# Expert layers: another router arithmetic, a first tile picked and last tiles joined on TensorE

## What is computed

```
# first mixture (L0): a router with a hidden layer, experts 512 -> 2048 -> 512
logits = silu(x @ rw1 + rb1) @ rw2 + rb2
k_prob = softmax(top_k(logits, 2))
out = sum_e we[e] * (silu(x @ w1[e] + b1[e]) @ w2[e] + b2[e])
# second mixture (L1): router_logits = x @ router_w + router_b, experts 512 -> 512 -> 512
ff_out = (silu(x @ we_gate[e]) * (x @ we_up[e])) @ we_down[e]
```

## Time and profile before

| | us |
|---|---|
| median of 3 runs | 2418.44 |
| lowest, highest | 2414.98, 2419.09 |
| the profiled execution's own time | 2414.82 |
| its span, first to last instruction | 2412.8 |
| TensorE busy | 2134.6 |
| TensorE's mean granted clock | 0.948 |

### The profile page before, as it was taken

The page is one execution under the profiler, slowest core; times in us unless marked ns, Lnnn a source line. Parts: engine busy times, 40 slices in busy tenths (PEclk is TensorE's granted clock), DMA queues, the critical chain, the costliest instruction groups (busy, mean ns, idle before and its releaser), DMA issues. The chain is left out here.

```text
span 2412.8 us, 37208 instructions
## 1 busy us (share of the span) xinstructions
PE 2134.6 (88%) x14521; PEld 1599.3 (66%) x14521; DVE 1382.4 (57%) x2318; ACT 1331.3 (55%) x2560; POOL 296.6 (12%) x268
## 2 busy tenths in 40 slices
PE   6999999999968957799999949999999999765895
PEld 4778787777735533278888736887787877532674
DVE  4455455454536651189999944544555545454686
ACT  2566566565624422088888824666665665401684
POOL 3111112121010000100000022121121121101001
PEclk9999999999988988799999969999999999978898
DMA  4010101010020013499999640010101010013896
GB/s 148 18 36 19 36 19 36 19 36 19 2 107 0 1 43 147 151 360 355 365 354 362 254 157 22 33 36 19 36 19 36 19 36 1 1 70 114 311 351 225
DMA packets 52220, 263.85 MB, mean 109 GB/s; under 512 B 9288, under 2 KB 9672, under 8 KB 25040
## 3 DMA queue, kind: packets, MB, share of 16 engines
q1 hardware_dynamic: 45168, 245.23, 27.4%
q0 software_dynamic: 2560, 8.39, 1.1%
q10 hardware_dynamic: 4320, 7.87, 0.9%
HBM read 244.42 MB, written 17.04 MB: 108 GB/s over the span
## 5 line engine op out<-in xcount | busy, mean ns | idle before, releaser
L508 DVE COPY c_pt<-bank 128x512 f32<-128x512 f32 x256 | 177.0, 692 | 548.9 <-PE bank L342 548.8
L658 ACT ACTIVATE c_pr<-wide,c_nmax 128x512 f32<-128x512 f32 x512 | 348.9, 696 | 164.7 <-DVE c_nmax L500 83.9
L231 POOL TENSOR_TENSOR c_clo<-c_raw,c_chi 128x512 fp32r<-128x512 f32 x128 | 167.3, 1311 | 991.9 <-ACT c_chi L635 991.9
L342 PE MATMUL bank<-ident,c_pr 128*128 128x128 f32 x2048 | 268.6, 273 | 13.9 <-DVE c_pt L508 11.8
L342 PEld LDWEIGHTS bank<-ident,c_pr 128*128 128x128 f32 x2048 | 238.0, 140 | 49.9 <-DVE c_pt L508 14.0
L92 PE MATMUL bank<-c_wv_hi,c_chi 128*128 128x512 f32 x512 | 218.4, 426 | 20.1 <-POOL c_clo L231 18.8
L643 ACT ACTIVATE c_khi<-bank,c_cols 128x512 fp32r<-128x512 f32 x128 | 87.9, 687 | 252.1 <-PE bank L94 252.1
L1535 DVE TENSOR_TENSOR moe_wlo<-moe_raw,moe_whi 128x2048 fp32r<-128x2048 f32 x97 | 219.4, 2286 | 12.7 <-ACT moe_whi L1426 12.5
L92 PE MATMUL bank<-c_chi,c_wk_hi 128*128 128x512 f32 x512 | 213.6, 417 | 8.7 <-ACT c_v L649 8.6
L1426 ACT CAST moe_whi<-moe_raw 128x2048 fp32r<-128x2048 f32 x97 | 185.3, 1931 | 37.0 <-DMA moe_raw<-in_L_ffn_w 14.2
L93 PE MATMUL bank<-c_wv_lo,c_chi 128*128 128x512 f32 x512 | 203.2, 397 | 0.0
(11 more groups left out here) (320 smaller groups left out, 3877.4 us busy)
## 6 DMA issues: line engine op xcount, KB each, us to landing
moe_hr<-in_L_ffn_w SPq DMA_DIRECT2D x68, 1024.0 KB, 7.2
moe_raw<-in_L_ffn_w SPq DMA_DIRECT2D x52, 1024.0 KB, 7.2
c_raw<-in_ctx SPq DMA_DIRECT2D x32, 1024.0 KB, 4.9
moe_raw<-in_L_ffn_we_gate SPq DMA_DIRECT2D x15, 1024.0 KB, 7.2
moe_raw<-in_L_ffn_we_up SPq DMA_DIRECT2D x15, 1024.0 KB, 7.5
moe_raw<-in_L_ffn_we_down SPq DMA_DIRECT2D x15, 1024.0 KB, 7.0
slot_outputs<-moe_ob ACTq DMA_DIRECT2D x30, 256.0 KB, 7.4
ret_w<-in_L_attn_w_attn SPq DMA_DIRECT2D x4, 1024.0 KB, 9.1
```

The source lines that it names most:

```text
L231: nc.gpsimd.tensor_tensor(clo[:, g % 2, c, :], raw[:, c, :], f32(chi[:, g % 2, c, :]), ALU.subtract) \
L342: last = pe.transpose(TB[n % 2][:, h * P:(h + 1) * P], pr[:, u % 2, h, n * P:(n + 1) * P], k["ident"][:])
L508: nc.vector.tensor_copy(pt[:, n, :], TB[0][:]).then_inc(pt_dve, 1)
L658: nc.scalar.activation(pr[:, u % 2, h, :], S[h][:], ACT.Exp, bias=nmax[:, b % 2, i, at:at + 1], scale=-1.0 if masked else 1.0, accum_out=d ...
```

## The change

- The zero rows of `slot_rows` are written in the retention stage, behind its own loads.
- First layer's router: `rw1` comes in four 1 MB parts among the first expert blocks; it and the turned rows are split into rounded part and remainder, and each full-precision matmul becomes three one-pass products (`hidden`).
- Logits: `rw2` is laid into columns padded from 8 to 32, and four hidden pieces are multiplied in four column groups of TensorE (`to_logits`), in the first layer four times, three of these between the hidden products. Four matmuls with a 0/1 matrix `fold` then add the groups and turn the result; the bias is added behind that.
- First tile: 0/1 matrices `here` (128 tokens by 128 slots) are made on VectorE and 16 full-precision matmuls put the first tile's turned rows straight into `XB` (`place_first`). The other 14 tiles still go through DRAM.
- Last tiles (`LATE`: one in the first layer, two in the second): their outputs stay in `ob`. GpSimd makes a matrix with each pair's probability at its slot, TensorE turns it in the loop (`turn_late`), and behind the loop full-precision matmuls with it add these tiles to the tokens (`join_late`), in the first layer with the b2 product. The gather takes only the earlier tiles (`EARLY`) and doesn't wait for the last; a pair of a late tile gathers row 0 with probability 0.
- VectorE's and TensorE's steps for b2 move from ahead of the first layer's loop into it.

```diff
                 sp.dma_start(wp[:], t["L0_attn_w_proj"]).then_inc(S["wp_in"], 16)
+                sp.wait_ge(S["zero"], 1)
+                sp.dma_start(slots.rearrange("(i p) d -> p i d", p=P), zero[:].to_broadcast([P, slots.shape[0] // P, D])) \
+                    .then_inc(S["zeroed"], 16)
+                sp.wait_ge(S["zeroed"], 16)
...
+    LATE = 1 if first else 2
+    EARLY = NT - LATE
...
+        RWN = 48 if first else 32
+        CHUNK = ((1, 3), (3, 7), (7, NT))
...
+                    rw1_of = t["L0_ffn_rw1"].rearrange("p c (g h) -> p g c h", g=GR)
+                    sp.dma_start(rw1[:, 0], rw1_of[:, 0]).then_inc(r1_in[0], 16)
...
-                    sp.dma_start(rw1, t["L0_ffn_rw1"]).then_inc(s_["rw_in"], 16)
+                    sp.dma_start(rw1[:, 1], rw1_of[:, 1]).then_inc(r1_in[1], 16)
...
+                    load(0)
+                    sp.dma_start(rw1[:, 2], rw1_of[:, 2]).then_inc(r1_in[2], 16)
+                    load(1)
+                    sp.dma_start(rw1[:, 3], rw1_of[:, 3]).then_inc(r1_in[3], 16)
                     sp.dma_start(b1[:], t["L0_ffn_b1"]).then_inc(s_["b_in"], 16)
                     sp.dma_start(b2[:], t["L0_ffn_b2"]).then_inc(s_["b_in"], 16)
+                    load(2)
+                    sp.wait_ge(s_["logits_made"], 1)
...
-                if first:
-                    sp.wait_ge(s_["filled"], 1)
-                    sp.dma_start(xg.rearrange("(i p) d -> p i d", p=P), hr[:, 0:1, :].to_broadcast([P, NT, D])) \
-                        .then_inc(s_["zeroed"], 16)
...
-                    sp.dma_start(rows_in[:, a:b, :], xg[a * P:b * P, :].rearrange("(i p) d -> p i d", p=P)).then_inc(xg_in[i], 16)
+                    sp.dma_start(rows_in[:, a - 1:b - 1, :], xg[a * P:b * P, :].rearrange("(i p) d -> p i d", p=P)).then_inc(xg_in[i], 16)
...
+                pool.wait_ge(s_["filled"], 1)
+                pool.wait_ge(s_["rw_in"], RWN)
+                nc.gpsimd.tensor_copy(rw2_wide[:, :, 0:NE], rw2[:]).then_inc(s_["wide"], 1)
...
+                pool.wait_ge(s_["scattered"], 16 * 2 * NB)
+                pool.wait_ge(x_turned, 1)
+                pool.wait_ge(s_["probs"], 1)
+                for l in range(LATE):
+                    for b in range(NB):
+                        for i, to in enumerate((late_of, late_2nd)):
+                            nc.gpsimd.tensor_scalar(to[:, l, b * P:(b + 1) * P], in_late[:, l, :], slot_f[:, b, i:i + 1],
+                                                    prob[:, b, i:i + 1], ALU.is_equal, ALU.mult).then_inc(s_["late_parts"], 1)
+                pool.wait_ge(s_["late_parts"], 2 * NB * LATE)
+                nc.gpsimd.tensor_tensor(late_of, late_of, late_2nd, ALU.add).then_inc(s_["late_made"], 1)
+                pool.wait_ge(od_done[0], 16 * ((EARLY + 1) // 2))
+                pool.wait_ge(od_done[1], 16 * (EARLY // 2))
...
-                    nc.gpsimd.indirect_dma_start(out=back[:, i, :], out_offset=None, in_=od,
-                                                 in_offset=bass.IndirectOffsetOnAxis(ap=slot_i[:, i:i + 1], axis=0)) \
+                    nc.gpsimd.indirect_dma_start(out=back[:, i, :], out_offset=None, in_=od[0:EARLY * P, :],
+                                                 in_offset=bass.IndirectOffsetOnAxis(ap=back_i[:, i:i + 1], axis=0)) \
...
+                def hidden(j):
+                    g, q = j // C, j % C
+                    if q == 0:
+                        pe.wait_ge(rlo_done, g + 1)
+                    after(pe, s_["h_read"], j - 1)
+                    for c in range(C):
+                        at = c * D + q * P
+                        last = three_products(pe, ps[4 + j % 2][:], whi[1][:, g % 2, at:at + P], wlo[1][:, g % 2, at:at + P],
+                                              xT_hi(c), xT_lo(c), c == 0, c == C - 1)
+                    last.then_inc(s_["h_made"], 1)
+
+                def to_logits(rows, g, n):
+                    if first:
+                        pe.wait_ge(s_["h_read"], C * (g + 1))
+                    for q in range(C):
+                        last = pe.matmul(ps[6][q * HD:(q + 1) * HD, :], rw2_wide[:, C * g + q, :], rows[:, C * g + q, :],
+                                         start=(g == 0), stop=(g == n - 1))
+                    return last
+
...
+                        hidden(j)
+                        if j == 2 * C - 1:
+                            pe.wait_ge(s_["wide"], 1)
+                        if j % C == C - 1 and j > C:
+                            to_logits(hr, j // C - 1, GR)
+                    last = to_logits(hr, GR - 1, GR)
+                else:
+                    pe.wait_ge(s_["wide"], 1)
+                    last = to_logits(xT, 0, 1)
                 last.then_inc(s_["logits_made"], 1)
+                pe.wait_ge(s_["folds"], 1)
...
-                    last = pe.transpose(ps[7][:, b * NE:(b + 1) * NE], logitT[:, b * P:(b + 1) * P], k["ident"][0:NE, 0:NE])
+                    last = pe.matmul(ps[7][:, b * NE:(b + 1) * NE], part[:, b * P:(b + 1) * P], fold[:], start=True, stop=True)
...
+                def place_first():
+                    pe.wait_ge(s_["here"], NB)
+                    for c in range(C):
+                        for b in range(NB):
+                            last = pe.matmul(XB[:, c * P:(c + 1) * P], xn[:, b, c * P:(c + 1) * P], here[:, b, :],
+                                             start=(b == 0), stop=(b == NB - 1))
+                    last.then_inc(x_turned, 1)
...
                     for b in range(NB):
-                        pe.matmul(ps[b][:], weT[:, b * P:(b + 1) * P], b2[:], start=True, stop=True).then_inc(s_["y_made"], 1)
-                pe.wait_ge(s_["slots"], 1)
+                        if first:
+                            pe.matmul(ps[b][:], weT[:, b * P:(b + 1) * P], b2[:], start=True, stop=False)
+                        for l in range(LATE):
+                            if b == 0:
+                                pe.wait_ge(out_kept, EARLY + l + 1)
+                            last = pe.matmul(ps[b][:], late_T[:, l, b * P:(b + 1) * P], ob[:, (EARLY + l) % 2, :],
+                                             start=(l == 0 and not first), stop=(l == LATE - 1))
+                        last.then_inc(s_["y_made"], 1)
...
-                turn_x(0)
+                place_first()
                 if first:
-                    pe.wait_ge(s_["y_added"], NB)
...
+                        if g == GR - 1:
+                            turn_weights()
+                        if g == 2 * GR:
+                            turn_late()
...
+                join_late()
...
+                def high_router(g):
+                    act.wait_ge(r1_in[g], 16)
+                    after(act, s_["h_made"], C * (g - 1))
+                    nc.scalar.copy(whi[1][:, g % 2, :].rearrange("p (c h) -> p c h", c=C), rw1[:, g]).then_inc(rhi_done, 1)
...
+                    for c in range(C):
+                        act.wait_ge(s_["turned"], c + 1)
+                        nc.scalar.copy(xT_hi(c), ps[4 + c % 2][:]).then_inc(s_["xThi"], 1)
+                    high_router(0)
+                    high_router(1)
...
+                        if j in (C - 1, 2 * C - 1):
+                            high_router(j // C + 2)
+                        if j in (2, C + 2):
+                            high(0, j // C)
+                    high(1, 0)
...
+                        if g >= 3 and (g - 3) % GR == GR - 1 and (g - 3) // GR < EARLY:
                             store((g - 3) // GR)
...
+                        if 1 <= g <= EARLY:
+                            store(g - 1)
...
-                    nc.vector.tensor_copy(xT[:, c, :], ps[4 + c % 2][:]).then_inc(s_["xT"], 1)
+                    if first:
+                        dve.wait_ge(s_["xThi"], c + 1)
+                        nc.vector.tensor_tensor(xT_lo(c), ps[4 + c % 2][:], f32(xT_hi(c)), ALU.subtract).then_inc(s_["xT"], 1)
...
+                def low_router(g):
+                    dve.wait_ge(rhi_done, g + 1)
+                    nc.vector.tensor_tensor(wlo[1][:, g % 2, :].rearrange("p (c h) -> p c h", c=C), rw1[:, g],
+                                            f32(whi[1][:, g % 2, :]).rearrange("p (c h) -> p c h", c=C), ALU.subtract) \
+                        .then_inc(rlo_done, 1)
...
+                    low_router(0)
+                    low_router(1)
...
-
-                dve.wait_ge(s_["rw_in"], 64 if first else 32)
+                    low_router(3)
+                nc.vector.tensor_reduce(fold[:], k["ident"][:].rearrange("p (g e) -> p e g", g=C)[:, 0:NE, :], AX.X, ALU.add) \
+                    .then_inc(s_["folds"], 1)
...
+                nc.vector.tensor_copy(part, ps[6][:]).then_inc(s_["logits_kept"], 1)
...
+                for b in range(NB):
+                    s.mark(nc.vector.tensor_scalar(here[:, b, :], in_tile[:], slot_f[:, b, 0:1], None, ALU.is_equal))
+                s.wait()
+                for b in range(NB):
```

(26 more changed lines are left out.)

169 lines of the change are left out of this document (92 added, 77 removed).

## The result

The changed kernel takes 2385.39 us (median of 4 runs, 2383.74 to 2385.86) against 2416.84 (2414.98 to 2419.09) before: a ratio of 0.9866, 95% interval 0.9852 to 0.9881. It is faster by 31.5 us, where 52.2 were predicted, and the time lies above the range (2345 to 2381). Its profiled execution took 2385.33 us (span 2383.6), 29.5 less than that of before.

What follows compares the result with a forecast made beforehand. TensorE, busy 88% of the span, was taken as the bound, with gains only where it waits or its work shrinks. First mixture -37.8 and second -14.4 gave -52.2, from 2414.8 to 2362.6 us; range 2345 to 2381.

Steps and rivals of the forecast that it cites:

- Router of the first mixture: First mixture, start to logits: logits at 963.1 against 995.5, so 32.4 us sooner.
- The rival in which the groups work in turn: Logits' column groups run one after the other, costing 10.3 and 2.7 us more: 2375.6 us, chance 0.08.
- First tiles: Slot numbers to early contractions: picking the first tile directly saves 4.9 us in the first mixture, 8.3 in the second.
- The stream rival: Weights and rows arrive as late after the slot numbers as before, losing both first-tile gains: 2375.8 us, chance 0.19.
- First mixture's loop: Turns of weights and late matrix, copies and small VectorE steps add 1.2 us once (0 to +5).
- First mixture's end: Earlier gather, then add_back, last output copy, 14-record join and last sum: 2.5 us sooner (-6 to +3).
- Second mixture, start to slot numbers: Second mixture's router: 8 records, 3.60, become 0.9 + 0.3, the fold adds 0.8: 1.6 us sooner.
- Second mixture's loop: Two late tiles turned with a ScalarE copy between them: 1.5 us added.
- Second mixture's end: Gather without the late tiles, add_back, then four sums, with TensorE's 16 records beside: 6.0 us sooner (-8 to 0).
- Slower than before: New operations shift the loop so TensorE idles each step and falls to its low clock; 2455 at 0.8, chance 0.03.
- The two that gave 2375.6 and 2375.8: Rivals: column groups working in turn (2375.6, chance 0.08); weight and row stream taking back both first tiles (2375.8, chance 0.19).

Runs made afterwards that it cites:

- b3: Changed kernel with the logits of both mixtures accumulated in one column group instead of four, without the sum over groups: 2399.68 us.
- c3: Changed kernel with the zero rows written in the first mixture again, on SyncE's queue behind the small tensors, the scatter waiting for them: 2386.31 us.
- c1: Changed kernel with the first tile of both mixtures fetched from DRAM behind the scatter and turned, instead of picked by 0/1 products: 2397.54 us.
- a4: Changed kernel with the first mixture's seven transfers of the extra tiles' b1 columns issued one by one between later weight blocks: 2386.84 us.
- b1: Changed kernel with the rows of tiles 7 to 14 issued four blocks later in the first mixture, six later in the second: 2380.16 us.
- a2: Changed kernel with the last tile's output copied before add_back instead of behind it, at the first mixture's end: 2373.83 us.
- a1: Changed kernel with the second mixture's turns and copies of the late matrix at step 8 instead of step 3: 2381.37 us.
- b2: Changed kernel with the second mixture's two late tiles turned and copied in separate steps, 8 and 9: 2375.49 us.
- a3: Changed kernel with the four b2 products of the first mixture's join put ahead of the late tile's four products: 2378.73 us.

## Why the prediction failed, point by point

- *Router of the first mixture, -32.4.* Right (-32.6). 192 records at 0.23, the groups of logits at 1.06 (predicted 1.26; the trace notes no idle time at the changes of form), the first product 15.0 behind the start, as put. b3 shows the column groups' share (10.3), c3 that the zero rows ask for nothing where they went. The rival in which the groups work in turn had the right price, 10.3 and 2.7, and did not occur.
- *First tiles, -4.9 and -8.3.* The mechanism is right, the size a little off: c1 gives -3.4 and -6.7, the second in the presence of the late matrix's wait. First products stand 10.2 and 9.5 us behind the slot numbers (9.6 and 9.5 predicted). The term that was too small is the landing of the eighth block: 4.8 us from its issue in my sum, 6.9 in the trace. The stream rival, too, is true in part: a4 and b1 show that the queue's bytes set that moment.
- *First mixture's loop, +1.2.* 2.2 by c1 against before (which includes the making of `here`).
- *First mixture's end, -2.5, measured +4.2.* Moved to the new scale, the steps up to the copy of the last output hold within a microsecond: first gather 1344.3 (1344.40), the copy done at 1364.1 (it ends at 1364.84). The mis-sized term is the join: "14 records behind it, 6.0 at the full clock and 8.0 with a low start" took 14.1. Of the 6.1 too much some 4 are the clock, which did not come back: 14 records in a row at the low clock, 0.85 each, would be 11.9. The other 2.1 are the products that take turns, 1.0 a record; at the full clock that would be 0.53, not 0.43. I took the low start from a row in which it came back after some 4 us.
- *Second mixture, start to slot numbers, -1.6, measured +0.5.* All of it ran at the low clock, where the kernel before had the full one: logits 1.94 (predicted 0.9 + 0.3), the eight small records of the sum over the groups 1.85, for 0.41 of turns before. In a2, with the same code, the logits caught the full clock (1.06).
- *Second mixture's loop, +1.5, measured +13.3 by c1.* This is the step that failed. I wrote that GpSimd's operations "are off the path unless they hold up VectorE" and for the second mixture counted turns and a copy only. It is TensorE that waits: `turn_late` stands in its order at step 3, and nobody had asked when the matrix is ready. a1 and b2 bring back 10.9 of it. In the 2.4 that are left b2 has a wait of TensorE of 2.35, behind the subtraction that GpSimd's sum held up, so the condition in my sentence came true too. The risk could be read before the change, though not the price, for which no row of before has a GpSimd operation of this form: 16 operations behind the second step's start, each longer wherever VectorE subtracts, as the scatter step of 2.57 in the earlier trace rows already showed.
- *Second mixture's end, -6.0.* -7.1.
- *The rivals.* "Slower than before" did not occur; from the second contraction to the last the first mixture's loop shows no idle gap of TensorE over 0.3 us. The two that gave 2375.6 and 2375.8 were nearest in time, for other reasons.

## What to carry to other kernels

An operation that is moved to an idle engine has a due time: find the first instruction of an in-order engine that waits for it, and work out when it is ready with the price it has beside the others' work, and look at what it does to theirs. A wait on two turns through one bank costs whatever the copying engine has queued ahead; spread them over steps. At the end of a loop, put first what releases the engine that has most left to do, reckon small joins at the low clock, and keep products of one kind in a row.

## What the runs showed of the hardware

- GpSimd's tensor_scalar of 128x128 takes 0.79 us alone, 2.91 or 5.02 where it meets one or two of VectorE's subtractions of two SBUF tensors (2.28 each). VectorE loses nothing by these (2.290 against 2.284). Gather and scatter steps show the same: 0.95 alone, 2.95 and 2.98 beside such a subtraction.
- A subtraction that starts beside GpSimd's sum of two tensors of 1024 elements, or while that sum waits, takes 4.41 to 4.54 us in six kernels, instead of 2.28.
- Full-precision products of 512 columns, each with new weights, take 0.86 us each at the full and 1.7 at the low clock in a row of one kind (second join, b2 products of a3), and 1.05 and 2.0 where products of 8 and of 128 rows take turns (a2, the kernel after).
- With TensorE busy without a gap, the granted clock stayed at 0.50 for 14 us in one kernel, and in another fell from 1.00 to 0.50 while it worked. The page's mean clock of the whole span (0.95 before and after) shows nothing of it.
- Four full-precision matmuls of 32 columns by 512 take 1.06 us in four column groups and 3.62 in one, at the full clock.
